# A new start of the graph kernel: another load order, the parameter chain on GpSimd, the weight sums on VectorE, and the first neighbour product in plain fp32

## What is computed

```python
xc = transpose(x)                                            # 16 x 128 x 512
h = relu(bn1(conv1(xc)))                                     # 1 tap, 128 -> 128
x_conv = relu(bn2(conv2(h)) + xc)                            # 17 taps
s = x @ w_se.T + b_se                                        # 3 columns
A = exp(-(sq_n + sq_m - 2 s s^T)) * adj                      # 512 x 512
x_nmp = A @ relu(x @ w_msg.T + b_msg)                        # the neighbour product
gi, gh = [x_conv, x_nmp] @ w_ih.T + b_ih, x @ w_hh.T + b_hh  # gates r, z, n
x = layernorm(x + (1 - z) * tanh(gi_n + r * gh_n) + z * x)
```

## Time and profile before

| | before |
|---|---|
| median of 3 runs | 405.14 us |
| profiled execution | 401.42 us |
| its span (first to last instruction) | 399.1 us |
| outside the span | 2.3 us |
| PE busy in the span | 374.6 us, 94% |
| VectorE busy | 355.7 us, 89% |
| ScalarE busy | 230.7 us, 58% |
| GpSimd busy | 41.5 us, 10% |
| mean granted TensorE clock | 0.981 |

### The profile page before, as it was taken

One profiled execution on the slowest core, in us unless ns is written; L12 is line 12 of the kernel. 1 busy time (PEld: TensorE's weight loads), 2 busy tenths in 40 slices (PEclk: granted clock), 3 DMA queues, 4 the chain that ended last, 5 costly groups with the idle time before them and its releaser, 6 DMA issues.

```text
span 399.1 us, 7030 instructions
## 1 busy us (share of the span) xinstructions
PE 374.6 (94%) x2263; PEld 326.7 (82%) x2263; DVE 355.7 (89%) x731; ACT 230.7 (58%) x356; POOL 41.5 (10%) x46
## 2 busy tenths in 40 slices
PE   3589899999999999999999999999999999899995
PEld 2478689898979797989898898989797979688783
DVE  4988779999999999999999999999999999986646
ACT  4355456747565665666665667475656754654450
POOL 4500002110010101010101010100101060101013
PEclk9988889999999999999999999999999999999999
DMA  7627040504122221404040504040312204000100
GB/s 196 213 56 210 1 132 11 157 3 140 27 71 93 65 94 38 129 4 154 10 158 0 158 10 149 9 137 25 97 66 69 89 12 132 2 26 2 30 29 21
DMA packets 27305, 30.17 MB, mean 76 GB/s; under 512 B 3086, under 2 KB 16326, under 8 KB 27286
## 3 DMA queue, kind: packets, MB, share of 16 engines
q1 hardware_dynamic: 27256, 29.92, 24.5%
q10 hardware_dynamic: 30, 0.01, 0.0%
HBM read 24.84 MB, written 4.40 MB: 73 GB/s over the span
## 4 chain that ended last, share of the span: by engine, by line
PE 63%; DVE 21%; issue 10%; ACT 4%; DMA 1%; DVEq 0%; SPq 0%; POOLq 0%; ACTq 0%; POOL 0%
PE p_outer L602 14%; PE ring L602 13%; PE p_middle L602 8%; PE p_r L602 8%; PE p_z L602 8%; PE p_gi L602 7%; PE p_gh L602 4%; DVE sd_l L1121 3%; DVE dd L1107 2%; DVE sd L1116 2%; DVE st L1198 2%; DVE m_l L1130 2%; DVE n_l L1281 2%; DVE sd L1117 1%; ACT rows L840 1%
## 5 line engine op out<-in xcount | busy, mean ns | idle before, releaser
L602 PE MATMUL p_middle<-sd_h,w_h 128*128 128x256 f32 x192 | 56.7, 295 | 0.0
L1010 POOL TENSOR_TENSOR rs<-base,cst 128x5 f32<-128x5 f32 x16 | 20.0, 1250 | 332.7 <-DVE base L1209 332.7
L602 PE MATMUL p_middle<-sd_h,w_l 128*128 128x256 f32 x192 | 54.4, 283 | 0.0
L602 PE MATMUL p_middle<-sd_l,w_h 128*128 128x256 f32 x192 | 54.1, 282 | 0.0
L602 PE MATMUL p_outer<-dd_h,w_h 128*128 128x256 f32 x176 | 50.0, 284 | 2.5 <-issue 2.5
L865 ACT ACTIVATE am<-ring 128x512 f32<-128x512 f32 x64 | 37.9, 595 | 24.7 <-PE ring L602 24.3
L602 PE MATMUL p_outer<-dd_h,w_l 128*128 128x256 f32 x176 | 50.2, 285 | 0.0
L602 PE MATMUL p_outer<-dd_l,w_h 128*128 128x256 f32 x176 | 50.0, 284 | 0.0
L1136 DVE TENSOR_TENSOR am<-am,adj 128x512 f32<-128x512 f32 x64 | 40.9, 683 | 2.9 <-ACT am L865 2.9
L1252 DVE TENSOR_TENSOR am_l<-am,am_h 128x2048 fp32r<-128x2048 f32 x16 | 36.7, 2293 | 3.7 <-ACT am_h L914 3.7
L602 PEld LDWEIGHTS p_outer<-dd_h,w_h 128*128 128x128 f32 x176 | 34.0, 193 | 3.8 <-issue 3.2
(11 more groups left out here) (288 smaller groups left out, 969.7 us busy)
## 6 DMA issues: line engine op xcount, KB each, us to landing
adj<-adjT SPq DMA_DIRECT2D x64, 256.0 KB, 3.3
xin<-xT SPq DMA_DIRECT2D x17, 256.0 KB, 2.8
out<-yo SPq DMA_DIRECT2D x16, 256.0 KB, 2.2
gw<-g_w SPq DMA_DIRECT2D x2, 640.0 KB
wc<-w_c SPq DMA_DIRECT2D x2, 384.0 KB, 4.7
right<-left SPq DMA_DIRECT2D x14, 48.0 KB
wg<-w_ih SPq DMA_DIRECT2D x1, 384.0 KB, 5.8
wc<-w_c SPq DMA_DIRECT2D x1, 320.0 KB, 3.6
```

Source lines behind the costliest of these rows:

```text
L602: return nc.tensor.matmul(out_, w, x, start=start, stop=stop, skip_group_check=True)
L1010: TT(rs[:], base[:], cst[:, C_MH:C_MH + CH + 1], ALU.pow).then_inc(s_rs, 1)
```

## The change

Batch 0 gets lists of its own, `first()` on PE, ScalarE and VectorE; the common `step` loses its special cases and starts with batch 1 (it is otherwise the same).

- Loads: x(1) second, taps w1 third, `cst` fourth; `vec`, the conv1 weight and `wrow` go through ScalarE's queue ahead of its first activation. `bd` ahead of `bmsg` and adj(0). The second `right` comes by a DMA out of `left`, as in later batches, not by VectorE.
- GpSimd: the parameter chain in ten small instructions, the power against a memset column (`half`) and not `cst`; one small copy; no weight work.
- VectorE: no parameter chain, but the three weight instructions that GpSimd had; batch 0 in another order.
- PE: the four first `dist` products go to four banks; conv1(1) and msg(1) stand before the `p_middle` work; degrees stand before the wait for `n_h`, `n_l`.
- The neighbour product of batch 0 is four plain fp32 matmuls of `m0` (ScalarE, into `zt`) and `am`. `am_h`, `am_l`, `m_h`, `m_l` of batch 0 are gone, with the counts of their waits one lower in all later batches.
- Adjacency: `bd` goes in without the identity; VectorE adds the selection when it copies the result (`sel1`, kept in `rt` and `nn`), where ScalarE copied before.

The core of the diff (eight columns of indentation cut):

```diff
--- before.py
+++ after.py
...
-sel1 = part(wc2, 0, 64, CC)
+sel1 = [t[0:64, 0:4 * CC].rearrange("p (j w) -> p j w", w=CC) for t in (rt, nn)]
+m0 = zt
...
-    sp.dma_start(wc1[:], w_c1[:, :]).then_inc(s_wc1d, 16)
-    sp.dma_start(vec[:], vecs[:, :]).then_inc(s_vec, 16)
+    sp.dma_start(xin[:, 1, :], xT[1, :, :]).then_inc(s_x[1], 16)
+    sp.dma_start(wc2[:, 0::3, :], w_c2[:, 0::3, :]).then_inc(s_w2d[0], 16)
     sp.dma_start(cst[:], consts[:, :]).then_inc(s_cst, 16)
-    sp.dma_start(wc2[:, 0::3, :], w_c2[:, 0::3, :]).then_inc(s_w2d[0], 16)
-    sp.dma_start(wmsg[:], w_msg[:, :]).then_inc(s_wmsgd, 16)
-    sp.wait_ge(s_zero, 1)
-    sp.dma_start(wrow[:, 64:128], w_rows[:, :]).then_inc(s_wrowd, 16)
     for q in range(2):
         sp.dma_start(brow[64 * q:64 * q + 64, :], b_rows[:, :]).then_inc(s_brow, 16)
-    sp.dma_start(xin[:, 1, :], xT[1, :, :]).then_inc(s_x[1], 16)
+    sp.dma_start(wmsg[:], w_msg[:, :]).then_inc(s_wmsgd, 16)
     sp.dma_start(wc2[:, 2::3, :], w_c2[:, 2::3, :]).then_inc(s_w2d[2], 16)
     sp.dma_start(wc2[:, 1::3, :], w_c2[:, 1::3, :]).then_inc(s_w2d[1], 16)
+    sp.wait_ge(s_zero, 4)
+    for q in range(2):
+        sp.dma_start(bd[SLOT * q:SLOT * q + GN, :, SLOT * q:SLOT * q + GN],
+                     adjT[q::2, 0:GN, 0:GN].rearrange("j m n -> m j n")).then_inc(s_bdd, 16)
     sp.dma_start(bmsg[:], b_msg[:, :].to_broadcast([128, D])).then_inc(s_bmsg, 16)
     for c in range(CH):
...
+    sp.wait_ge(s_left, 1)
+    sp.dma_start(full(right[1][64:64 + KD, :]), full(left[96:96 + KD, :])).then_inc(s_right[1], 16)
...
-    pe.wait_ge(s_xh, 1); pe.wait_ge(s_xl, 1); pe.wait_ge(s_w1s, 2)
-    conv1(0)
-    pe.wait_ge(s_wmsgd, 16)
-    msg(0, FIRST_MSG)
-    pe.wait_ge(s_w1s, 4); pe.wait_ge(s_xh, 2); pe.wait_ge(s_xl, 2)
-    rows(0)
...
+    def first():
+        pe.wait_ge(s_xh, 1); pe.wait_ge(s_w1s, 1)
+        mm(R_C1[:], wc1_h[:], x_h[0][:], True, False)
+        pe.wait_ge(s_w1s, 2)
+        mm(R_C1[:], wc1_l[:], x_h[0][:], False, False)
+        pe.wait_ge(s_xl, 1)
+        mm(R_C1[:], wc1_h[:], x_l[0][:], False, True).then_inc(s_c1, 1)
+        pe.wait_ge(s_w1s, 4); pe.wait_ge(s_xh, 2); pe.wait_ge(s_xl, 2)
+        rows(0)
+        pe.wait_ge(s_wmsgd, 16)
+        msg(0, FIRST_MSG)
+        pe.wait_ge(s_ddh, 1); pe.wait_ge(s_ddl, 1); pe.wait_ge(s_whi, 1); pe.wait_ge(s_wlo, 1)
+        conv_part(p_outer[:, 0:HALF], w1_h, w1_l, dd_h, dd_l, 0)
+        pe.wait_ge(s_left, 1); pe.wait_ge(s_right[0], 16); pe.wait_ge(s_h1, 1); pe.wait_ge(s_mt, 1)
+        for c in range(CH):
+            mm(FIRST_D[c][:], left[:, D * c:D * c + D], right[0][:]).then_inc(s_d[c], 1)
+        pe.wait_ge(s_whi, 2); pe.wait_ge(s_wlo, 2)
+        conv_part(p_outer[:, HALF:N], w4_h, w4_l, dd_h, dd_l, 1).then_inc(s_outer, 1)
+        pe.wait_ge(s_e[0], 1)
+        conv1(1)
+        pe.wait_ge(s_e[1], 1)
+        msg(1, R_MSG)
+        spread_rows()
+        pe.wait_ge(s_sdh, 1); pe.wait_ge(s_sdl, 1); pe.wait_ge(s_whi, 3); pe.wait_ge(s_wlo, 3)
+        conv_part(p_middle[:, HALF:N], w3_h, w3_l, sd_h[:, 1], sd_l[:, 1], 1)
+        pe.wait_ge(s_whi, 4); pe.wait_ge(s_wlo, 4)
+        conv_part(p_middle[:, 0:HALF], w2_h, w2_l, sd_h[:, 0], sd_l[:, 0], 1).then_inc(s_middle, 1)
+        pe.wait_ge(s_m0, 1); pe.wait_ge(s_mt, 2)
+        for c in range(CH):
+            pe.wait_ge(s_am[c], 1)
+            last = mm(R_NMP[:], m0[:, D * c:D * c + D], am[:, c, :], c == 0, c == CH - 1)
+        last.then_inc(s_nmp, 1)
+        pe.wait_ge(s_left, 1); pe.wait_ge(s_right[1], 16); pe.wait_ge(s_h1, 2)
+        dist(1, 0)
+        spread_columns()
+        pe.wait_ge(s_wgs, 2); pe.wait_ge(s_e[2], 1)
+        gate(p_r, "r", 2, x_h[0], x_l[0], True, False)
+        pe.wait_ge(s_e[3], 1)
+        gate(p_z, "z", 2, x_h[0], x_l[0], True, False)
+        pe.wait_ge(s_ac, 2)
+        gate(p_gh, "n", 2, x_h[0], x_l[0], True, True).then_inc(s_gx, 1)
+        degrees()
+        pe.wait_ge(s_nh, 1); pe.wait_ge(s_nl, 1)
+        dist(1, 1)
+        gate(p_r, "r", 1, n_h, n_l, False, False)
+        pe.wait_ge(s_e[0], 2)
+        dist(1, 2)
+        gate(p_z, "z", 1, n_h, n_l, False, False)
+        pe.wait_ge(s_dg, 1)
+        gate(p_gi, "n", 1, n_h, n_l, True, False).then_inc(s_gn, 1)
+        pe.wait_ge(s_e[1], 2)
+        dist(1, 3)
+        pe.wait_ge(s_ch, 1); pe.wait_ge(s_cl, 1)
+        gate(p_r, "r", 0, c_h, c_l, False, True).then_inc(s_gr, 1)
+        gate(p_gi, "n", 0, c_h, c_l, False, True).then_inc(s_gi, 1)
+        gate(p_z, "z", 0, c_h, c_l, False, True).then_inc(s_gz, 1)
...
+    def first():
+        act.dma_start(vec[:], vecs[:, :]).then_inc(s_vec, 16)
+        act.dma_start(wc1[:], w_c1[:, :]).then_inc(s_wc1d, 16)
+        act.dma_start(wrow[:, 64:128], w_rows[:, :]).then_inc(s_wrowd, 16)
+        z = Fixed(0)
+        x_high(0, z, 0)
+        x_high(0, z, 1)
+        act.wait_ge(s_zero, 3); act.wait_ge(s_prm, 5)
+        first_conv(z, 0)
+        act.wait_ge(s_w2d[0], 16)
+        A(w1_h[:], wc2[:, 0::3, :], ACT.Copy).then_inc(s_whi, 1)
+        differences_high(z, 0)
+        act.wait_ge(s_w2d[2], 16)
+        A(w4_h[:], wc2[:, 2::3, :], ACT.Copy).then_inc(s_whi, 1)
+        act.wait_ge(s_rowb, 1)
+        act.wait_ge(s_rows, 1)
+        A(ab, p_gh[:], ACT.Identity, bias=rowb[:, 0:1], scale=cst[:, C_ROW:C_ROW + 1]).then_inc(s_ab, 1)
+        act.wait_ge(s_val, 1)
+        A(val_h[:], val, ACT.Copy).then_inc(s_valh, 1)
+        act.wait_ge(s_mt, 1)
+        A(m0[:], mt[:], ACT.Relu).then_inc(s_m0, 1)
+        sums_high(z, 0)
+        act.wait_ge(s_wsum, 3)
+        A(w3_h[:], wsum[:, 1], ACT.Copy).then_inc(s_whi, 1)
+        for c in range(CH):
+            act.wait_ge(s_d[c], 1)
+            A(am[:, c, :], FIRST_D[c][:], ACT.Exp).then_inc(s_e[c], 1)
+            if c == 1:
+                act.wait_ge(s_wsum, 4)
+                A(w2_h[:], wsum[:, 0], ACT.Copy).then_inc(s_whi, 1)
+        first_conv(z, 1)
+        act.wait_ge(s_wgd, 32)
+        A(wg_h[:], wg[:], ACT.Copy).then_inc(s_wgs, 1)
+        x_high(0, z, 2)
+        act.wait_ge(s_mt, 2)
+        A(m_h[1][:], mt[:], ACT.Relu).then_inc(s_mh, 1)
+        differences_high(z, 1)
+        act.wait_ge(s_prm, 7)
+        conv_sums(z)
+        sums_high(z, 1)
+        conv_out(z)
+        neighbours(z)
+        for c in range(CH):
+            act.wait_ge(s_d[c], 2); act.wait_ge(s_nmp, 1)
+            A(am[:, c, :], R_D[c][:], ACT.Exp).then_inc(s_e[c], 1)
+            if c == 0:
+                gate_n(z)
+        act.wait_ge(s_fw, 2)
+        A(fe[:], fw[:], ACT.Exp, bias=fs[:, 1:2], accum_out=fs[:, 2:3]).then_inc(s_fe, 1)
+        gates(z)
...
+    nc.gpsimd.memset(half[:], -0.5).then_inc(s_zero, 1)
+    nc.gpsimd.memset(wrow[:, 0:64], 0.0)
+    nc.gpsimd.memset(wrow[:, 128:192], 0.0).then_inc(s_zero, 1)
+    nc.gpsimd.memset(h1[:, 0:PAD], 0.0)
     nc.gpsimd.memset(h1[:, PAD + N:], 0.0).then_inc(s_zero, 1)
+    nc.gpsimd.memset(bd[:], 0.0).then_inc(s_zero, 1)
     for q in range(2):
         nc.gpsimd.memset(full(right[q][:]), 0.0).then_inc(s_zero, 1)
-    nc.gpsimd.memset(bd[:], 0.0).then_inc(s_zero, 1)
+        nc.gpsimd.memset(yo[q][:, 0, 0:1], 0.0).then_inc(s_out[q], 16)
+
+    pool.wait_ge(s_vec, 16); pool.wait_ge(s_zero, 1)
+    TS(prm[:, P_VE:P_VE + 2], vec[:, V_V1:V_V2 + 1:4], EPS, None, ALU.add).then_inc(s_prm, 1)
+    pool.wait_ge(s_prm, 1)
+    TT(prm[:, P_RS:P_RS + 2], prm[:, P_VE:P_VE + 2], half[:], ALU.pow).then_inc(s_prm, 1)
+    pool.wait_ge(s_prm, 2)
+    TT(prm[:, P_S1:P_S1 + 2], vec[:, V_G1:V_G2 + 1:4], prm[:, P_RS:P_RS + 2], ALU.mult).then_inc(s_prm, 1)
+    pool.wait_ge(s_prm, 3)
+    TT(prm[:, P_T1:P_T1 + 2], vec[:, V_M1:V_M2 + 1:4], prm[:, P_S1:P_S1 + 2], ALU.mult).then_inc(s_prm, 1)
+    pool.wait_ge(s_prm, 4)
+    TT(prm[:, P_A1:P_A1 + 2], vec[:, V_B1:V_B2 + 1:4], prm[:, P_T1:P_T1 + 2], ALU.subtract).then_inc(s_prm, 1)
+    TT(prm[:, P_R:P_R + 2], vec[:, V_IR:V_IR + 2], vec[:, V_HR:V_HR + 2], ALU.add)
+    TS(prm[:, P_H2:P_H2 + 1], prm[:, P_S2:P_S2 + 1], 0.5, None, ALU.mult)
+    TS(prm[:, P_N2:P_N2 + 1], prm[:, P_S2:P_S2 + 1], -1.0, None, ALU.mult)
+    TS(prm[:, P_HB:P_HB + 1], vec[:, V_HN:V_HN + 1], 0.5, None, ALU.mult).then_inc(s_prm, 1)
+    pool.wait_ge(s_prm, 6)
+    TS(prm[:, P_RH:P_RH + 2], prm[:, P_R:P_R + 2], 0.5, None, ALU.mult).then_inc(s_prm, 1)
+    pool.wait_ge(s_w2d[0], 16)
+    nc.gpsimd.tensor_copy(wsum[:, 0, G3 - 1:G3, :], wc2[:, TAPS - 2:TAPS - 1, :]).then_inc(s_wsum, 1)
     nc.gpsimd.memset(x1[:], 0.0).then_inc(s_zero, 1)
...
-    pool.wait_ge(s_w2d[0], 16)
-    nc.gpsimd.tensor_copy(wsum[:, 0, G3 - 1:G3, :], wc2[:, TAPS - 2:TAPS - 1, :])
-    pool.wait_ge(s_w2d[2], 16)
-    TT(wsum[:, 0, 0:G3 - 1, :], wc2[:, 0:TAPS - 2:3, :], wc2[:, 2::3, :], ALU.add).then_inc(s_wsum, 1)
-    pool.wait_ge(s_whi, 2)
-    TT(w4_l[:], wc2[:, 2::3, :], full(w4_h[:]), ALU.subtract).then_inc(s_w4l, 1)
-    pool.wait_ge(s_w2d[1], 16); pool.wait_ge(s_wsum, 1)
-    TT(wsum[:, 1], wsum[:, 0], wc2[:, 1::3, :], ALU.subtract).then_inc(s_wsum, 1)
...
+    def first():
```

(80 more changed lines are left out.)

328 lines of the change are left out of this document (87 added, 241 removed).

## The result

The changed kernel takes **388.85 us** (median of 4 runs, 387.35 to 390.41), against 405.23 for the kernel before on the same chip (4 runs, 403.12 to 406.61). The ratio is 0.9601, with a 95% interval of 0.9536 to 0.9665. Its profiled execution took 387.58 us with a span of 385.8, against 401.42 and 399.1 before. The forecast of 394.1 was too high by 5.25 us, and its range of 391.3 to 398.0 did not hold the result.

The account below looks back on a forecast made before the run. Batch 1's start was taken as the bound: 8.4 + 25.8 + 2.0 + 5.1 = 41.3, 43.0 with the clock term, against 53.98. The 11.0 us off the 405.14 median gave 394.1 us, range 391.3 to 398.0.

Parts of the forecast that it names:

- the clock term: On PE's last piece before batch 1: one half-clock stretch of 3.4 us, costing +1.7 us (bounds 0 and +3.6).
- the base: Whole kernel: the 11.0 us gain was taken off the median 405.14, which stood 3.7 above the profiled execution.
- T1: The time batch 1 starts on PE: forecast 43.0 with the clock term, against 53.98 before.
- the clock holds: Rival, chance 0.20: work before PE's last piece is dense enough to keep the clock up; 392.7 us.
- last piece: Second half of batch 0's gates on PE, up to T1: 5.1 us in place of 9.8, -4.7.
- The start of `dd`: First large VectorE piece after `h1`: starts at 8.4 and not 11.73, -3.3 us (bounds -4.2 and -1.2).
- the list: VectorE's work from `dd` to `cv` ready: 25.8 us in place of 30.5, -4.7 (bounds -2.7 and -5.1).
- the handover: From `cv` through `c_h`, `n_h`, `n_l` to PE: stays at 2.0 us.
- batch 1: From batch 1's start on PE to batch 2: 22 us, as before.
- The mechanism named for `dd`: VectorE instructions with two SBUF inputs and GpSimd instructions reading SBUF exclude each other, so GpSimd's weight work held up VectorE.
- PE's cover: PE through its list at 33.7, before `n_l` at 36: 2.4 us to spare, enough for one half-clock stretch.
- The other rivals: Clock low twice or more (0.14), VectorE's list head waiting (0.14), VectorE bound in batch 1 (0.07), slower (0.03).

Follow-up runs that it names:

- before: The kernel before, unchanged, in its first profile: profiled execution 401.42 us, span 399.1; median 405.23 us.
- b_same: The kernel before run again, no edit: 400.17 us (12 runs), ratio 0.9989.
- b_dve: The kernel before with the three weight instructions moved from GpSimd to VectorE: 400.38 us, ratio 0.996.
- a_deg: The changed kernel with the 16 degree matmuls put back behind the wait for `n_l`: 392.05 us, ratio 0.9728 to the kernel before.
- b_fill: The kernel before with 24 unread 512-column matmuls in PE's four gaps of batch 0: 398.0 us, ratio 0.9925.
- a_gap: The changed kernel with the degrees moved behind batch 0's last gate, leaving the gap open: 390.32 us, ratio 0.9777 to the kernel before.
- after: The first profile of the changed kernel: profiled execution 387.58 us, span 385.8; median 388.85 us.
- b_deg: The kernel before with only the 16 degree matmuls moved ahead of the wait for `n_l`: 398.42 us against 402.46, ratio 0.9935.
- a_same: The changed kernel run again, no edit: 389.47 us (five runs), ratio 0.9696 to the kernel before.
- a_pool: The changed kernel with the three long weight instructions back on GpSimd: 394.74 us, ratio 0.9807 to the kernel before.
- a_split: The changed kernel with batch 0's neighbour product in split precision again, 12 matmuls: 393.9 us, ratio 0.9785 to the kernel before.
- a_loads: The changed kernel with all first loads on SyncE in the old order: 391.4 us, ratio 0.9743 to the kernel before.
- a_best: The changed kernel with `x_low` and `msg_low` behind `conv_sum` and `spread_rows` earlier on PE: 388.33 us, ratio 0.9699 to the kernel before.
- a_cols: a_best with `spread_columns` also ahead of the neighbour product: 387.14 us (6 runs), ratio 0.963 to the kernel before.

## Why the prediction was wrong, step by step

**The steps that failed** are two. The first is the clock term, "I expect one low stretch of 3.4 us on it: +1.7". Measured: 0; the clock is 1.00 from 7.65 to 40.66. The second is the base: the shift was taken off a median that stood 3.7 us above the profiled execution, and 2.9 of the 5.25 us lie there and outside the span (worked out below). With the measured T1 the prediction's own sum gives 405.14 - 13.3 = 391.8, inside its range; what took the result out of the range is the second.

For the clock the bound 0 was named, and "the clock holds" was a rival with 0.20, at 392.7. The reason given for +1.7, that the columns spread, the degrees and a gap "lie right before this piece", was read off, where gap, degrees and fall stand together. The experiments set them apart, for this piece:

| | gap ahead, us | degrees inside | last piece | clock |
|---|---|---|---|---|
| before, b_same, b_dve, a_deg | 1.75 to 1.86 | yes | 9.8 | down to 0.50 |
| b_fill | filled | yes | 6.5 | 1.00 |
| a_gap | 1.75 | no | 5.1 | 1.00 |
| after, b_deg | 0.35, 0.56 | no | 5.1 | 1.00 |

What is shown: with the degrees ahead of the wait and the gap cut to 0.35 or less the clock held on this piece in every profile that has this order, after and a_same, a_pool, a_split, a_loads, a_best and a_cols. The forecast counted on a gap of 1 to 2 us behind the degrees; it was 0.35, because PE's list took 1.9 us more than its prices (below). So the clock may have held in part because another term was wrong; no run here has this order with a longer gap.

What is not shown is why the clock falls. The pair of gap and degrees went with the fall in four profiles, but a_deg also had a run at a mean clock of 0.999; in a_deg's profile the clock was down as the degrees began; and in a_split, and at the first fall of the earlier trace rows (18.75, behind 2.5 us of idle PE and eleven matmuls of 256 columns at full clock), it fell with no small matmuls behind the gap. Behind the end of the gap the fall came after 1.2 us in a_deg, 1.5 to 2.1 in before, b_same and b_dve, and at once in a_split. That the moment of the gap decides, and not what stands behind it, is a rival that no run here tests.

**The start of `dd`** was mis-sized: 7.65 for 8.4, a term of -4.1 for -3.3, within its bounds. `cst` landed at 6.9, not at 8.3 (4.8 us from issue to landing), so the loads newly ahead of it cost 1.0 and not 2.4. `vec` landed at 3.8 and not 4.4. The parameters were ready at 6.15 (6.4 forecast), of the small kind throughout (0.19 to 0.72), and `h1` ran at 6.80 behind PE, not behind them.

**The other terms** held: the list 25.9 (25.8), the handover 2.0 (2.0), the last piece 5.1 (5.1), batch 1 22.0 (22). VectorE passed no lag on: its last mask ends at 40.3 and `gg` at 40.9, as PE starts batch 1 at 40.66. The mechanism named for `dd` held as well (a_pool, a_loads), though b_deg and b_fill show that the held instruction is another from one execution to the next: with the weight work still on GpSimd `dd` started at 9.76 and 9.77 there, so some 2 us of its gain over 11.73 hang on the execution that was profiled.

**PE's cover** was thinner than forecast, 0.35 for 2.4. PE was through the degrees at 35.2 and not 33.7. Its waits were as forecast (1.6 for `mt` and 0.5 for the first exponential, for some 2) and it began its list at 10.8 for 11.3; but the list took 22.3 and not 20.4, each block a little more than its price, the degrees most (1.57 for 1.1). It cost nothing here.

**Taking the shift off the median** is the second step that failed. Of the 5.25 us between forecast and result 2.34 lie in T1 (the clock 1.7, the start 0.75, the rest -0.1). 0.5 lie outside the span, 2.3 before and 1.8 after; that difference shows in every kernel built from the one or the other but b_dve, where it is 1.8 in half of the runs, and its cause is open. The last 2.4 are in the base. The median before stood 3.7 above the profiled execution and the one after stands 1.3 above its own, while the sum was made from profiled executions, and the range left 0.5 for the spread of the runs, which is 7.7 us in b_same. With more runs the difference of the medians is 10.7 (b_same and a_same) and that of the shortest spans 11.6: less than the 13.3 of the profiled pair, as T1 varies too: 46.79 to 54.67 in the profiles of the kernel before and its versions.

The other rivals did not come about: no instruction at the head of VectorE's list waited more than 0.47 for a load, and batches 1 and on were not slower.

## What to carry to other kernels

A start that is paid once is worth splitting into landmarks, and each landmark's stretch can be compared with its steady twin in a later batch: what the twin doesn't have (4.7 us here) is what can be had. A block of small matmuls that does not need what TensorE waits for is best moved into that wait; one block of 16 gave about a fifth of the gain here (0.65% of 3.0%), its own time and the clock's together. Where the granted clock falls differently from run to run, a forecast should be tied to the profiled execution, and the range for the median should hold the few microseconds that the falls are worth.

## What was not expected of the hardware

The same 20 matmuls took 2.36 or 4.1 us from one execution to the next of the same kernel, by the granted clock alone, and with them the span moved by 3 to 5 us. GpSimd's small instructions on 128x1 and 128x2 vary more than their size: 0.19 to 0.58 for the same product or scalar form, and 0.72 for the power. And where VectorE and GpSimd meet, either can be the one that is held. In a_pool VectorE was, 2.06 and 1.99 in place of 0.70 and 0.75; `rows` between them kept its 0.75, but one of its inputs, `p_gh`, is not in SBUF. In b_fill it was GpSimd, whose first long piece took 3.98 for 1.53, while `dd`, both halves of `sd` and `dd_l` beside it took 0.70 each:

```profile
9.79 3.98 POOL L1027 TENSOR_TENSOR yy<-wc 128x640 f32<-128x640 f32 x1 [2.61 <-DMA wc<-w_c]
```
